# All 32 down products of a gated expert layer as split products, with GpSimd making four low parts, under new stage orders

## The chip, the cores and the metric

The kernel runs on one core of one Trainium2 chip. The metric is the device time of one execution in microseconds (us); lower is better. The engines are named as in the profile: PE (TensorE), PEld (its weight loads), DVE (VectorE), ACT (ScalarE), POOL (GpSimd) and SP (the queue that issues DMAs).

## The reference, cut to what matters

Four sequences of 256 tokens with 128 features pass through gated cross-attention (2 heads of 64, 256 context tokens of 96 features, the latents appended to keys and values), and then through a gated expert layer with a residual. The second part is what the change touches:

```python
def ffn(x, expert_sel, keys, values):            # x: normalised, 1024 tokens x 128
    sel_logits = jnp.einsum('nd,ed->ne', xt, expert_sel)
    gates = jax.nn.sigmoid(sel_logits)
    sel_val, sel_idx = jax.lax.top_k(gates, 4)   # of 32 experts
    gate_full = jnp.zeros_like(gates).at[jnp.arange(N)[:, None], sel_idx].set(sel_val)
    scores = jax.nn.relu(jnp.einsum('nd,edf->nef', xt, keys))      # 32 experts x 64
    scores = scores * gate_full[:, :, None]
    return jnp.einsum('nef,efv->nv', scores, values)
x = x + tanh(g_xattn) * xattn(ctx, layernorm(x), mask, ...)
x = x + tanh(g_ffn) * ffn(layernorm(x), expert_sel, keys, values)
```

Every gate is computed, all 32 experts are evaluated for all tokens, and gates outside the top four are zero.

## The kernel before, in words

Each engine runs one list of stages in the written order (`PE_ORDER`, `POOL_ORDER`, `DVE_ORDER`, `ACT_ORDER`); stages are tied together by semaphores. A stage name is followed by its index: a sequence (0 to 3) for `turn_in 2` or `select 3`, sequence and part for `row_max 1.0`, half and chunk for `up 0.7` and `down 1.3`.

**Attention.** For each sequence: statistics and normalisation (`stats_in`, `norm_in`, on DVE and ACT), transposes (`turn_in`), projections (`project`), per-head norms of queries and keys (`sum_qk`, `norm_qk`), transposes back (`turn_qk`, and on ACT rounded copies, `round_qk`), the score maxima (`row_max`: PE makes scores, DVE reduces them), the maxima moved to rows (`turn_max`), exponentials (`weights`: scores on PE, Exp on ACT), the weighted values (`attend`, two tiles per sequence), and on DVE the residual (`out_proj`), statistics and normalisation (`stats_mid`, `norm_mid`, `turn_mid`). `warm` is a matmul on an identity whose result nobody reads. `constants` on ACT makes a bf16 identity and the open part of the mask.

**Gates.** `select` makes 32 logits per token (PE), the top four and sigmoids (DVE), `turn_gates` transposes them (PE, ACT), and SP writes them to DRAM and reads each row back, broadcast over 64 partitions, into one of 6 slots (`gated`), one load per chunk.

**Expert layer.** The 2048 hidden columns are 16 chunks of 128, and the tokens two halves of 512: 32 chunks, n = 16*half + chunk. `up` on PE is a product of split operands: `product` adds low x high, high x low and high x high in three fp32r matmuls of 512 columns (L729, L730, L731). `up` on DVE (L543) applies ReLU and gate and writes the fp32 chunk to one of 3 slots of `hid`. For n >= WHOLE = 4, ACT's `split` (L706) writes its rounded high part `hid_hi` and DVE's `split` (L560) the difference `hid_lo`, in rings of 4 slots, and `down` is again a `product` with `v_hi`, `v_lo`. For n < 4 `down` is one plain fp32 matmul on `hid` (L921), which shows as two instructions. DVE may not overwrite a `hid` slot before the three older chunk's down product (n < 4) or both its parts (n >= 4) are done:

```python
def free_hid(n):
    if 0 <= n < WHOLE:
        dve.wait_ge(down_done, n + 1)
    elif n >= WHOLE:
        dve.wait_ge(hid_hi_ready, n - WHOLE + 1)
        dve.wait_ge(hid_lo_ready, n - WHOLE + 1)
```

PE's `up` uses three PSUM banks in turn, so `up` n waits for DVE's `up` n-3. `turn_res` adds the residual into the accumulator by a transpose before the first `down` of a half.

**POOL** makes the low parts of keys and values, four quarters each (L349), the mask (L344) and the biased residual (`add_bias`, L363). In the attention part the orders are written out by hand, as everywhere.

Of the kernel before, what the change touches and what calls it, by code (L numbers as in the profile page):

```python
# [33 lines left out]
WHOLE = 4
# [32 lines left out]
    select 3, up 0.11, down 0.7, up 0.12, down 0.8, up 0.13, turn_gates 3, down 0.9, up 0.14, up 0.15, down 0.10,  # L67
    down 0.11, up 1.0, up 1.1, down 0.12, turn_res 2, down 0.13, up 1.2, down 0.14, turn_res 3, up 1.3,
    down 0.15, up 1.4, up 1.5, down 1.0, up 1.6, down 1.1, up 1.7, up 1.8, down 1.2, down 1.3, up 1.9, down 1.4,
    down 1.5, down 1.6, up 1.10, up 1.11, down 1.7, up 1.12, up 1.13, down 1.8, down 1.9, up 1.14, up 1.15,  # L70
    down 1.10, down 1.11, down 1.12, down 1.13, down 1.14, down 1.15
# [4 lines left out]
"""
DVE_ORDER = """
    stats_in 0, norm_in 0, stats_in 1, scale_wo 0, norm_in 1, stats_in 2, sum_qk 0, norm_in 2, stats_in 3,
    norm_qk 0, sum_qk 1, norm_in 3, norm_qk 1, row_max 0.0, row_max 0.1, row_max 1.0, turn_max 0, sum_qk 2,
    row_max 1.1, norm_qk 2, sum_qk 3, turn_max 1, norm_qk 3, row_max 2.0, row_max 2.1, row_max 3.0, out_proj 0,  # L80
    turn_max 2, stats_mid 0, row_max 3.1, norm_mid 0, out_proj 1, turn_max 3, stats_mid 1, turn_mid 0,
# [10 lines left out]
    stats_in 0, norm_in 0, constants 0, stats_in 1, turn_in 0, norm_in 1, fold 0, project 0, stats_in 2,  # L92
    turn_in 1, sum_qk 0, vctx 0, vlat 0, norm_in 2, project 1, split_keys 0, turn_in 2, stats_in 3, vlat 1,
    turn_qk 0, sum_qk 1, round_qk 0, norm_in 3, vctx 1, turn_in 3, turn_qk 1, round_qk 1, vlat 2, vctx 2,
    split_keys 1, project 2, split_values 0, vlat 3, sum_qk 2, vctx 3, weights 0.0, project 3, turn_qk 2,
    sum_qk 3, round_qk 2, weights 0.1, split_keys 2, weights 1.0, turn_qk 3, round_qk 3, weights 1.1,
    split_keys 3, stats_mid 0, weights 2.0, weights 2.1, turn_mid 0, stats_mid 1, weights 3.0, select 0,
    turn_mid 1, split_values 1, turn_gates 0, select 1, weights 3.1, turn_gates 1, stats_mid 2, turn_mid 2,
    split_values 2, split_values 3, stats_mid 3, select 2, split 0.4, split 0.5, split 0.6, split 0.7,
    turn_mid 3, split 0.8, split 0.9, select 3, split 0.10, turn_gates 2, turn_gates 3, split 0.11, split 0.12,  # L100
    split 0.13, split 0.14, split 0.15, split 1.0, split 1.1, split 1.2, split 1.3, finish 0, split 1.4,
# [898 lines left out]
```

## Time and profile before

| what | value |
|---|---|
| median of 3 runs | 114.44 us (114.16 to 114.53) |
| the profiled execution | 113.83 us, of which the span is 112.0 us |
| busy of the span | PE 105.6, DVE 94.4, ACT 65.1, POOL 16.0 us |
| granted TensorE clock, mean | 0.995 of full |

The span runs from the first to the last instruction; 1.83 us of the profiled execution lie outside it. Busy shares are averages over two parts with different limits: the attention part ends at about 60.5 us with the last `attend`, the expert layer fills the rest.

### The profile page before, as it was taken

The numbers are of one execution on the slowest core, as the hardware profiler recorded it, in microseconds if no ns is written. First come the engines' busy times: TensorE is split into PE (matmuls) and PEld (weight loads), VectorE is DVE, ScalarE is ACT, GpSimd is POOL, SyncE is SP. The second block draws the span as 40 slices with busy tenths as digits, with TensorE's granted clock in tenths as the row PEclk, the third lists the DMA queues.
The fourth block names the chain that finished last, engine by engine and source line by source line (L and its number), as shares of the span: only waits on it lengthen the run. The fifth ranks groups of instructions, "written<-read, shape, count | busy, mean of one in ns | idle before, by whom it ended". The sixth has DMA issues, their size and how long they took to land.

```text
span 112.0 us, 2072 instructions
## 1 busy us (share of the span) xinstructions
PE 105.6 (94%) x644; PEld 85.4 (76%) x644; DVE 94.4 (84%) x307; ACT 65.1 (58%) x145; POOL 16.0 (14%) x27
## 2 busy tenths in 40 slices
...
DMA packets 7111, 12.78 MB, mean 114 GB/s; under 512 B 893, under 2 KB 2557, under 8 KB 6846
## 3 DMA queue, kind: packets, MB, share of 16 engines
...
HBM read 12.00 MB, written 0.66 MB: 113 GB/s over the span
## 4 chain that ended last, share of the span: by engine, by line
PE 79%; DVE 8%; ACT 7%; issue 3%; POOL 0%; DVEq 0%; POOLq 0%
PE bank L729 13%; PE bank L731 13%; PE bank L730 13%; PE bank L867 12%; PE bank L738 6%; PE bank L854 5%; PE bank L921 3%; PE bank L825 2%; DVE junk L453 2%; PE bank L852 2%; PE bank L788 2%; PE bank L813 1%; ACT cx L600 1%; PE bank L807 1%; PE bank L892 1%
## 5 line engine op out<-in xcount | busy, mean ns | idle before, releaser
L706 ACT ACTIVATE hid_hi<-keys 128x512 fp32r<-128x512 f32 x28 | 17.5, 630 | 18.5 <-DVE keys L543 15.3
L543 DVE SCALAR_TENSOR_TENSOR keys<-bank,inT 128x512 f32<-128x512 f32 x32 | 21.1, 685 | 1.3 <-issue 0.6
L560 DVE TENSOR_TENSOR hid_lo<-keys,hid_hi 128x512 fp32r<-128x512 f32 x28 | 18.7, 685 | 0.9 <-ACT hid_hi L706 0.6
L867 PE MATMUL bank<-vw,prob 128*128 128x129 f32 x128 | 15.8, 278 | 0.0
L867 PEld LDWEIGHTS bank<-vw,prob 128*128 128x128 f32 x128 | 14.8, 192 | 0.7 <-issue 0.7
L729 PE MATMUL bank<-xm_hi,k_lo 128*128 128x512 f32 x32 | 14.5, 454 | 0.0
L453 DVE CUSTOM_DVE_ANT_0 junk<-bank,mask_b 128x512 bf16<-128x512 f32 x16 | 10.4, 688 | 3.0 <-PE bank L825 3.0
L731 PE MATMUL bank<-xm_hi,k_hi 128*128 128x512 f32 x32 | 12.5, 391 | 0.0
L730 PE MATMUL bank<-xm_lo,k_hi 128*128 128x512 f32 x32 | 12.5, 390 | 0.0
L729 PE MATMUL bank<-hid_hi,v_lo 128*128 128x512 f32 x28 | 11.2, 399 | 0.0
L731 PE MATMUL bank<-hid_hi,v_hi 128*128 128x512 f32 x28 | 10.9, 391 | 0.0
L730 PE MATMUL bank<-hid_lo,v_hi 128*128 128x512 f32 x28 | 10.9, 390 | 0.0
L674 ACT ACTIVATE prob<-bank 128x512 f32<-128x512 f32 x16 | 8.6, 592 | 3.5 <-PE bank L854 3.4
L738 PE MATMUL bank<-ident 128*128 128x128 f32 x48 | 8.3, 327 | 1.5 <-POOL ident L330 1.5
L349 POOL TENSOR_TENSOR k_lo<-keys,k_hi 128x512 fp32r<-128x512 f32 x4 | 5.1, 1271 | 30.7 <-ACT k_hi L642 30.7
L738 PEld LDWEIGHTS bank<-ident 128*128 128x128 f32 x48 | 7.8, 241 | 1.7 <-POOL ident L330 1.5
L854 PE MATMUL bank<-qT,kT 64*128 64x256 f32 x64 | 9.1, 375 | 0.0
L729 PEld LDWEIGHTS bank<-xm_hi,k_lo 128*128 128x128 f32 x32 | 6.0, 188 | 2.0 <-issue 0.7
L730 PEld LDWEIGHTS bank<-xm_lo,k_hi 128*128 128x128 f32 x32 | 6.0, 189 | 1.9 <-issue 1.0
L349 POOL TENSOR_TENSOR v_lo<-values,v_hi 128x512 fp32r<-128x512 f32 x4 | 5.1, 1275 | 16.9 <-ACT v_hi L648 16.9
L731 PEld LDWEIGHTS bank<-xm_hi,k_hi 128*128 128x128 f32 x32 | 6.0, 188 | 1.3
L731 PEld LDWEIGHTS bank<-hid_hi,v_hi 128*128 128x128 f32 x28 | 5.3, 188 | 1.1
...
## 6 DMA issues: line engine op xcount, KB each, us to landing
...
```

What stands on the lines that cost most here:

```text
L349: pool.tensor_tensor(lo[:, part], src[:, part], hi[:, part].bitcast(F32), ALU.subtract).then_inc(lo_ready, 1)
L453: dve.tensor_tensor_reduce(junk[:, n % 2, :], bank_of(b, ROW_MAX + i)[:, :], mask_b[:, b, :], 1.0, SENTINEL, ALU.add, ALU.max, mx[:, b, i ...
L543: dve.scalar_tensor_tensor(hid[:, n % 3, :], bank[H_BANK[n % len(H_BANK)]][:, :], 0.0, gated[:, n % SLOTS, :], ALU.max, ALU.mult).then_inc ...
L560: dve.tensor_tensor(hid_lo[:, m % RING, :], hid[:, n % 3, :], hid_hi[:, m % RING, :].bitcast(F32), ALU.subtract).then_inc(hid_lo_ready, 1)
L674: act.activation(prob[:, b % 2, a, 2 * i:2 * i + 2, :], head_bank(b, a)[:, :].rearrange("p (t s) -> p t s", t=2), ACT.Exp).then_inc(prob_r ...
L706: act.activation(hid_hi[:, m % RING, :], hid[:, n % 3, :], ACT.Copy).then_inc(hid_hi_ready, 1)
L729: pe.matmul(o, ll, rh, start=start, stop=False)
L730: pe.matmul(o, lh, rl, start=False, stop=False)
L731: return pe.matmul(o, lh, rh, start=False, stop=stop)
L738: pe.matmul(bank[5][:, 0:P], ident[:, :], ident[:, :], start=True, stop=True)
L854: last = pe.matmul(o[a], kT[rows[a], b, keys_t], qT[rows[a], b, :], start=False, stop=True)
L867: last = pe.matmul(bank_of(b, OUT + t)[:, WOA * a:WOA * a + WOA], prob[:, b % 2, a, j, P * t:P * t + P], vw[:, b, j, a, :], start=(j == 0) ...
```

## The change: every chunk is split, and four low parts move to POOL

`WHOLE` becomes 0, so chunks 0.0 to 0.3 also get high and low parts and a three-matmul product. POOL makes the low part of every eighth chunk (0.5, 0.13, 1.5, 1.13), counted by a semaphore of its own; `wait_low` picks the semaphore. DVE thus makes 28 low parts as before, but two more of them in the first half and two fewer in the second. All four orders are new.

```diff
-WHOLE = 4
+POOL_EVERY, POOL_SLOT = 8, 5
+WHOLE = 0
...
+        def wait_low(engine, m):
+            pool_made = (m - POOL_SLOT) // POOL_EVERY + 1
+            if m % POOL_EVERY == POOL_SLOT:
+                engine.wait_ge(pool_lo_ready, pool_made)
+            else:
+                engine.wait_ge(hid_lo_ready, m + 1 - pool_made)
...
+            def split(h, c):                                  # gpsimd
+                n = EC * h + c
+                m = n - WHOLE
+                pool.wait_ge(hid_ready, n + 1)
+                pool.wait_ge(hid_hi_ready, m + 1)
+                if m >= RING:
+                    pool.wait_ge(down_done, n - RING + 1)
+                pool.tensor_tensor(hid_lo[:, m % RING, :], hid[:, n % 3, :], hid_hi[:, m % RING, :].bitcast(F32),
+                                   ALU.subtract).then_inc(pool_lo_ready, 1)
...
-                    dve.wait_ge(hid_lo_ready, n - WHOLE + 1)
+                    wait_low(dve, n - WHOLE)
...
-                    pe.wait_ge(hid_lo_ready, m + 1)
+                    wait_low(pe, m)
```

The parts of the orders that matter below (before, then after):

```diff
 PE_ORDER
-    turn_in 0, warm 13, warm 14, warm 15, warm 16, warm 17, warm 18, fold 0, project 0, turn_in 1, warm 19,
-    vlat 0, vctx 0, warm 20, project 1, turn_in 2, vctx 1, warm 21, vlat 1, warm 22, turn_qk 0, warm 23, vctx 2,
-    vlat 2, turn_in 3, row_max 0.0, turn_qk 1, vlat 3, row_max 0.1, row_max 1.0, project 2, turn_max 0, vctx 3,
-    row_max 1.1, weights 0.0, project 3, turn_max 1, turn_qk 2, weights 0.1, weights 1.0, row_max 2.0, turn_qk 3,
-    attend 0.0, row_max 2.1, weights 1.1, row_max 3.0, attend 0.1, turn_max 2, attend 1.0, row_max 3.1,
-    weights 2.0, attend 1.1, weights 2.1, turn_max 3, turn_mid 0, weights 3.0, select 0, attend 2.0, turn_mid 1,
-    weights 3.1, turn_gates 0, select 1, attend 2.1, turn_gates 1, attend 3.0, attend 3.1, turn_mid 2, up 0.0,
-    up 0.1, select 2, turn_res 0, turn_res 1, up 0.2, down 0.0, up 0.3, up 0.4, down 0.1, up 0.5, down 0.2,
-    up 0.6, down 0.3, up 0.7, up 0.8, down 0.4, turn_mid 3, down 0.5, turn_gates 2, up 0.9, down 0.6, up 0.10,
...
+    warm 13, turn_in 0, warm 14, warm 15, warm 16, warm 17, project 0, fold 0, warm 18, turn_in 1, warm 19,
+    vlat 0, project 1, vctx 0, turn_in 2, warm 20, warm 21, turn_qk 0, warm 22, vlat 1, vctx 1, row_max 0.0,
+    warm 23, vlat 2, vctx 2, row_max 0.1, turn_in 3, project 2, turn_qk 1, vctx 3, turn_max 0, vlat 3,
+    weights 0.0, row_max 1.0, project 3, weights 0.1, row_max 1.1, turn_qk 2, attend 0.0, turn_max 1, attend 0.1,
+    weights 1.0, row_max 2.0, turn_qk 3, weights 1.1, row_max 2.1, row_max 3.0, attend 1.0, turn_max 2,
+    row_max 3.1, attend 1.1, weights 2.0, turn_max 3, turn_mid 0, weights 2.1, weights 3.0, select 0, turn_mid 1,
+    attend 2.0, select 1, weights 3.1, attend 2.1, turn_gates 0, turn_gates 1, attend 3.0, attend 3.1, up 0.0,
+    turn_mid 2, up 0.1, select 2, turn_res 0, up 0.2, up 0.3, turn_res 1, down 0.0, up 0.4, up 0.5, down 0.1,
+    up 0.6, turn_gates 2, down 0.2, down 0.3, up 0.7, turn_mid 3, down 0.4, up 0.8, up 0.9, down 0.5, down 0.6,
...
+    up 1.14, down 1.10, up 1.15, down 1.11, down 1.12, down 1.13, down 1.14, down 1.15
 POOL_ORDER (after)
+    scale_bo 0, low_keys 0, mask 0, add_bias 0, low_values 0, low_keys 1, low_keys 2, low_keys 3, add_bias 1,
+    low_values 1, low_values 2, split 0.5, low_values 3, split 0.13, split 1.5, split 1.13
 DVE_ORDER
-    stats_mid 3, up 0.0, up 0.1, up 0.2, select 2, up 0.3, up 0.4, norm_mid 3, split 0.4, up 0.5, up 0.6, up 0.7,
...
+    stats_in 0, norm_in 0, stats_in 1, scale_wo 0, norm_in 1, stats_in 2, sum_qk 0, norm_in 2, norm_qk 0,
+    sum_qk 1, stats_in 3, row_max 0.0, norm_in 3, norm_qk 1, row_max 0.1, turn_max 0, sum_qk 2, row_max 1.0,
...
+    stats_mid 3, up 0.0, up 0.1, up 0.2, split 0.0, split 0.1, up 0.3, split 0.2, select 2, up 0.4, split 0.3,
+    norm_mid 3, up 0.5, split 0.4, up 0.6, turn_mid 3, up 0.7, split 0.6, up 0.8, up 0.9, split 0.7, split 0.8,
 ACT_ORDER (after)
+    stats_in 0, constants 0, norm_in 0, turn_in 0, stats_in 1, project 0, norm_in 1, fold 0, turn_in 1,
...
+    turn_qk 2, split_values 0, split_keys 3, round_qk 2, weights 1.0, turn_qk 3, round_qk 3, weights 1.1,
+    stats_mid 0, weights 2.0, turn_mid 0, stats_mid 1, weights 2.1, split_values 1, turn_mid 1, weights 3.0,
```

## Rows read from the trace of the kernel before

**Rows 1.** Busy time of each engine over the span, from the page.
```profile
PE 105.6 (94%) x644; PEld 85.4 (76%) x644; DVE 94.4 (84%) x307; ACT 65.1 (58%) x145; POOL 16.0 (14%) x27
```

**Rows 2.** One five-us stretch: length, busy PE, PEld, DVE, ACT, POOL, clock, DMA.
```profile
65.00:70.00 5.00, 5.00 (x19) 3.27 (x18) 4.72 (x20) 0.89 (x2) 0.00 (x0) 1.00 0.75 249
```

**Rows 3.** PE in order of time: start, length, line (idle before in brackets).
```profile
10.51 0.38 PE L746 MATMUL bank<-ident,xn 128*128 128x128 f32 x2
...
20.86 0.42 PE L749 MATMUL bank<-ident,cx 128*96 128x128 f32 x2 [0.49 <-ACT cx L600]
...
35.01 1.95 PE L867 MATMUL bank<-vw,prob 128*128 128x129 f32 x16
...
56.65 0.40 PE L892 MATMUL bank<-ident,gate 128*32 128x128 f32 x2 [0.38 <-DVE gate L534]
56.88 3.74 PE L867 MATMUL bank<-vw,prob 128*128 128x129 f32 x32
60.49 0.59 PE L875 MATMUL bank<-ident,xn 128*128 128x128 f32 x2
```

**Rows 4.** DVE in order of time, at the start of the expert layer.
```profile
63.05 1.26 DVE L543 SCALAR_TENSOR_TENSOR keys<-bank,inT 128x512 f32<-128x512 f32 x2
64.65 0.69 DVE L543 SCALAR_TENSOR_TENSOR keys<-bank,inT 128x512 f32<-128x512 f32 x1 [0.34 <-PE bank L731]
65.26 0.21 DVE L522 TENSOR_SCALAR logit<-bank 128x64 f32<-128x64 f32 x1
...
67.33 1.28 DVE L543 SCALAR_TENSOR_TENSOR keys<-bank,inT 128x512 f32<-128x512 f32 x2
68.53 0.15 DVE L496 SCALAR_TENSOR_TENSOR rs_mid<-rs_mid 128x2 f32<-128x2 f32 x1
...
69.63 0.69 DVE L560 TENSOR_TENSOR hid_lo<-keys,hid_hi 128x512 fp32r<-128x512 f32 x1
70.23 2.01 DVE L543 SCALAR_TENSOR_TENSOR keys<-bank,inT 128x512 f32<-128x512 f32 x3
72.16 1.28 DVE L560 TENSOR_TENSOR hid_lo<-keys,hid_hi 128x512 fp32r<-128x512 f32 x2
```

**Rows 5.** PE in order of time, in the expert layer.
```profile
69.79 1.02 PE L921 MATMUL bank<-keys,values 128*128 128x512 f32 x2
70.25 0.79 PE L729 MATMUL bank<-xm_hi,k_lo 128*128 128x512 f32 x1
70.88 0.40 PE L730 MATMUL bank<-xm_lo,k_hi 128*128 128x512 f32 x1
...
72.98 0.47 PE L729 MATMUL bank<-hid_hi,v_lo 128*128 128x512 f32 x1
...
101.32 0.39 PE L729 MATMUL bank<-xm_hi,k_lo 128*128 128x512 f32 x1
...
102.00 0.39 PE L729 MATMUL bank<-hid_hi,v_lo 128*128 128x512 f32 x1
```

**Rows 6.** ACT in order of time: an exponential pair, a rounded part, and the copies after key transposes.
```profile
36.24 0.71 ACT L661 ACTIVATE kT<-bank,vecs_x 128x512 f32<-128x512 f32 x1
36.81 0.45 ACT L665 ACTIVATE qT_hi<-qT 128x256 fp32r<-128x256 f32 x1
37.12 0.66 ACT L667 ACTIVATE kT_hi<-kT 128x512 fp32r<-128x512 f32 x1
38.53 1.09 ACT L674 ACTIVATE prob<-bank 128x512 f32<-128x512 f32 x2 [0.76 <-PE bank L854]
```

**Rows 7.** POOL in order of time: the mask, and two low parts of values.
```profile
17.62 1.04 POOL L344 TENSOR_SCALAR mask_b<-mask_u 128x1024 bf16<-128x1024 uint8 x1
...
62.10 2.52 POOL L349 TENSOR_TENSOR v_lo<-values,v_hi 128x512 fp32r<-128x512 f32 x2 [7.52 <-ACT v_hi L648]
```

**Rows 8.** DVE in order of time, beside the mask and after it.
```profile
17.65 1.02 DVE L384 SCALAR_TENSOR_TENSOR rs_in<-rs_in 128x4 f32<-128x4 f32 x1
...
19.69 0.17 DVE L384 SCALAR_TENSOR_TENSOR rs_qk<-rs_qk 128x12 f32<-128x12 f32 x1
```

More of the change, by code:

```diff
@@ L67 @@
[L67 to L71, printed above, removed]
+    warm 13, turn_in 0, warm 14, warm 15, warm 16, warm 17, project 0, fold 0, warm 18, turn_in 1, warm 19,
@@ new lines @@
+    attend 2.0, select 1, weights 3.1, attend 2.1, turn_gates 0, turn_gates 1, attend 3.0, attend 3.1, up 0.0,
+    turn_mid 2, up 0.1, select 2, turn_res 0, up 0.2, up 0.3, turn_res 1, down 0.0, up 0.4, up 0.5, down 0.1,
+    up 0.6, turn_gates 2, down 0.2, down 0.3, up 0.7, turn_mid 3, down 0.4, up 0.8, up 0.9, down 0.5, down 0.6,
+    up 0.10, down 0.7, select 3, up 0.11, up 0.12, down 0.8, up 0.13, turn_gates 3, up 0.14, down 0.9,
+    turn_res 2, turn_res 3, up 0.15, down 0.10, up 1.0, down 0.11, down 0.12, up 1.1, down 0.13, down 0.14,
@@ L72 @@
+    up 1.2, up 1.3, down 0.15, up 1.4, up 1.5, up 1.6, down 1.0, down 1.1, down 1.2, up 1.7, up 1.8, up 1.9,
+    down 1.3, down 1.4, up 1.10, down 1.5, up 1.11, down 1.6, down 1.7, down 1.8, up 1.12, up 1.13, down 1.9,
+    up 1.14, down 1.10, up 1.15, down 1.11, down 1.12, down 1.13, down 1.14, down 1.15
 """
 POOL_ORDER = """
-    low_keys 0, mask 0, low_keys 1, low_keys 2, scale_bo 0, add_bias 0, low_keys 3, add_bias 1, low_values 0,
-    low_values 1, low_values 2, low_values 3
+    scale_bo 0, low_keys 0, mask 0, add_bias 0, low_values 0, low_keys 1, low_keys 2, low_keys 3, add_bias 1,
@@ L76 @@
+    low_values 1, low_values 2, split 0.5, low_values 3, split 0.13, split 1.5, split 1.13
 """
 DVE_ORDER = """
[L78 to L81, printed above, removed]
@@ L87 @@
-    split 1.4, up 1.6, up 1.7, split 1.5, split 1.6, up 1.8, split 1.7, up 1.9, split 1.8, up 1.10, split 1.9,
-    up 1.11, split 1.10, up 1.12, up 1.13, split 1.11, split 1.12, up 1.14, up 1.15, split 1.13, split 1.14,
+    stats_in 0, norm_in 0, stats_in 1, scale_wo 0, norm_in 1, stats_in 2, sum_qk 0, norm_in 2, norm_qk 0,
+    sum_qk 1, stats_in 3, row_max 0.0, norm_in 3, norm_qk 1, row_max 0.1, turn_max 0, sum_qk 2, row_max 1.0,
+    norm_qk 2, sum_qk 3, row_max 1.1, norm_qk 3, turn_max 1, out_proj 0, row_max 2.0, stats_mid 0, row_max 2.1,
@@ new lines @@
+    row_max 3.0, norm_mid 0, turn_max 2, row_max 3.1, out_proj 1, stats_mid 1, turn_max 3, turn_mid 0,
+    norm_mid 1, turn_mid 1, select 0, select 1, out_proj 2, stats_mid 2, norm_mid 2, out_proj 3, turn_mid 2,
+    stats_mid 3, up 0.0, up 0.1, up 0.2, split 0.0, split 0.1, up 0.3, split 0.2, select 2, up 0.4, split 0.3,
+    norm_mid 3, up 0.5, split 0.4, up 0.6, turn_mid 3, up 0.7, split 0.6, up 0.8, up 0.9, split 0.7, split 0.8,
+    up 0.10, select 3, up 0.11, split 0.9, up 0.12, split 0.10, up 0.13, split 0.11, split 0.12, up 0.14,
@@ L91 @@
 ACT_ORDER = """
[L92 to L101, printed above, removed]
@@ L102 @@
-    split 1.5, split 1.6, split 1.7, split 1.8, split 1.9, split 1.10, split 1.11, split 1.12, split 1.13,
-    split 1.14, split 1.15
+    stats_in 0, constants 0, norm_in 0, turn_in 0, stats_in 1, project 0, norm_in 1, fold 0, turn_in 1,
+    stats_in 2, vlat 0, sum_qk 0, norm_in 2, split_keys 0, project 1, vctx 0, turn_qk 0, round_qk 0, turn_in 2,
+    sum_qk 1, stats_in 3, vlat 1, vlat 2, norm_in 3, vctx 1, vctx 2, turn_in 3, project 2, turn_qk 1, round_qk 1,
+    vctx 3, vlat 3, weights 0.0, sum_qk 2, project 3, weights 0.1, split_keys 1, split_keys 2, sum_qk 3,
@@ new lines @@
+    turn_qk 2, split_values 0, split_keys 3, round_qk 2, weights 1.0, turn_qk 3, round_qk 3, weights 1.1,
+    stats_mid 0, weights 2.0, turn_mid 0, stats_mid 1, weights 2.1, split_values 1, turn_mid 1, weights 3.0,
+    select 0, select 1, weights 3.1, split_values 2, turn_gates 0, turn_gates 1, stats_mid 2, turn_mid 2,
+    split 0.0, split 0.1, split 0.2, stats_mid 3, split 0.3, select 2, split 0.4, split 0.5, turn_mid 3,
+    split 0.6, split_values 3, split 0.7, split 0.8, split 0.9, select 3, split 0.10, turn_gates 2, turn_gates 3,
@@ L104 @@
+    split 0.11, split 0.12, split 0.13, split 0.14, split 0.15, split 1.0, split 1.1, split 1.2, split 1.3,
+    finish 0, split 1.4, split 1.5, split 1.6, split 1.7, split 1.8, split 1.9, split 1.10, split 1.11,
+    split 1.12, split 1.13, split 1.14, split 1.15
 """
```

11 lines of the change are left out of this document (5 added, 6 removed).

## The prediction, on record before the change was run

> **What bounds the kernel now.** First the page: PE is busy for 105.6 of 112.0 us and DVE for 94.4 [rows 1], so PE sets the end, with DVE close behind. The chain that ended last agrees: 79% of it is PE. POOL's 16.0 us leave room. Then PE in order of time. Up to the last `attend` (60.49) the idle times it shows are few: 0.49 us before the fourth `turn_in`, 0.38 before `turn_gates 1` [rows 3]. But its stages are worth less than the time they take: from 10.51 to 35.01, 24.5 us, their own costs add up to 21.8. I add 0.42 for a `turn_in`, 1.32 `project`, 0.87 `vlat` or `vctx`, 0.66 `turn_qk`, 0.46 `row_max`, 1.1 `weights`, 0.22 `warm`, each the distance between two starts in that timeline. So 2.7 us there are waits, written or smeared. From 35.01 to 60.49, 25.5 us, they add up to 24.4: 1.1 of waits.
>
> In the expert layer PE is full. A split product takes 0.68 us (101.32 to 102.00 [rows 5]); from 72.98, where `down 0.5` starts, to the end of the last product, 50 products (34.1) and four small stages fill everything. DVE has 0.60 us per chunk and operation (three in 70.23 to 72.16 are 1.93 with one handoff, pairs 1.20), and is 94% busy from 65 to 70 [rows 2]. `select` takes it 2.07 us (65.26 to 67.33), `norm_mid` 1.10 (68.53 to 69.63) [rows 4].
>
> **The change part by part.**
>
> *Four plain products become split.* The pair at 69.79 and the two matmuls behind it end the count at 70.88: 1.09 us, less 0.23 for one split matmul, is 0.86 [rows 5]. A split product is 0.68. PE gains 4 x 0.18 = 0.72 us. ACT gains 4 x 0.63 us of work, hidden, since it is mostly idle there.
>
> *DVE at the head of the expert layer.* This is what pays for it. DVE starts `up 0.0` at 63.05, after `out_proj 3`, `turn_mid 2` and `stats_mid 3`, all of them behind the last `attend`; the order of these is kept, so the distance (60.49 to 63.05) stays. `up 0.2` waits for PE today (0.34 us) and starts at about 64.5. From there the new order is a row of work with nothing to wait for until `split 0.4`: `up 0.2`, splits 0.0 and 0.1, `up 0.3`, split 0.2, `select 2`, `up 0.4`, split 0.3, `norm_mid 3`, `up 0.5`, split 0.4: nine operations at 0.60, 2.07 and 1.10, 8.6 us, and `split 0.4` is out at 73.15. PE needs it for `down 0.4` and starts that at 73.25. Behind it lie 28 down and 24 up products and four small stages (`select 3`, `turn_gates 3`, two `turn_res`). Before, PE had at 72.98 [rows 5] 27 down and 23 up products and five small stages behind it. So the new order is two products (1.36) minus one `turn_gates` (0.2) plus the 0.27 between 72.98 and 73.25 later: 1.4 us, the 0.72 included. Walked on PE, these are waits of 0.65 before `down 0.0` (it now needs a low part made behind `up 0.2`, where the plain product needed only `hid`), 0.5 before `turn_gates 2`, 0.2 before `down 0.3`, 0.7 before `down 0.4`, 0.2 more before `select 2`. After that DVE has spare room: by `up 1.3` the slot that PE asks for is 2 us old.
>
> *Late gate rows.* `turn_gates 3` comes at about 81.5 instead of 80.2, and the third load of the second half then lands near 90.3; the first product that needs it, `up 1.5`, starts at 92. Hidden, with 1 us of cover.
>
> *POOL's four low parts.* 2.52 us for two today [rows 7], so 1.27 each after ACT's 0.63: `split 0.5` is out about 2.0 us after `up 0.5`. DVE wants the slot for `up 0.8` 2.75 us after it (four operations and `turn_mid 3`), and 2.4 to 3.0 us later for the other two: hidden, cover 0.4 to 1.0 us. The trace has one warning. While POOL made the mask, DVE's `norm_in 3`, a 4-column operation on two SBUF inputs, took 1.02 us and ended with the mask; the like took 0.17 at 19.69 [rows 7, 8]. While POOL made low parts of values from 62.10 to 64.62, DVE's `up 0.0` and `up 0.1`, with one input in PSUM, kept 0.6 [rows 4, 7]. DVE's `split` reads two SBUF tensors, and no trace row shows it beside POOL. Bounds: 0, or four times 1.27 = 5.1 us of DVE. I take 0.3 us of DVE in the first half, covered by the 2 us of spare room there, and 0 on PE.
> The Trainium skill, "SBUF — State Buffer", section "Who interferes with whom", says that a DVE instruction with two SBUF inputs and a GpSimd instruction that reads SBUF exclude each other for a whole instruction. The 1.02 us agrees. By it each meeting costs one side up to an instruction; it speaks against moving these parts to GpSimd.
>
> *POOL's new queue.* `low_values 0` stands ahead of `low_keys 1` to `3` and waits for ACT's `split_values 0` (about 33.5); then five operations end at 39.8. The first reader of the last, `add_bias 1`, is `out_proj 2` (55), and `select 0` on ACT wants the keys' low parts at 49. Hidden. SP's list is unchanged.
>
> *The attention orders, first stretch (10.5 to `attend 0.0`).* `constants` goes ahead of `norm_in 0` on ACT and into the idle time there; `project 0` starts near 8.0 instead of 9.2, but `fold` (0.88) now follows it, so that only 0.1 is won by `turn_in 1`. The rest comes from `norm_qk 0` ahead of `stats_in 3` on DVE (13.65 instead of 15.04), so `turn_qk 0` and its rounding end at 17.7 instead of 20.0, and `row_max 0.0` goes at 18.0 instead of 21.2, ahead of `turn_in 3`. PE then has, up to `attend 0.0`, its own 21.8 us less 2.35 for stages that come later (`weights 1.0`, `row_max 2.0`, `turn_qk 3`, `turn_max 1`) and about 0.8 of waits: `attend 0.0` near 30.7.
>
> *Second stretch.* From there 24.4 + 2.35 own, and two new waits. `attend 1.0` needs `weights 1.1`, on ACT behind `turn_qk 3` and `round_qk 3`: after PE's transposes at 36.8, 0.95 + 0.8 + 1.08 [rows 6] is 39.6, PE is there at 39.0: 0.55. `weights 2.1` used to stand behind `attend 1.1`; now only `turn_max 3` and `turn_mid 0` separate it from `weights 2.0`, whose exponentials take 1.08 [rows 6]: 0.8. The 0.38 before `turn_gates 1` [rows 3] goes, as `select 1` comes ahead of `weights 3.1`. With 0.3 of small waits the last `attend` ends at 59.2 against 60.5: 1.3 us won.
>
> *Sum.* 112.0 - 1.3 + 1.4 = 112.1 of span. The profiled execution was 113.83, so 113.9 in its terms; the median of the runs shown is 114.44, 0.6 higher, and the forecast as such a median is 114.5. A measurement here tells about 0.3% (0.34 us) from no change.
>
> **The rivals.**
>
> *A: the attention orders win more.* My walk is long, and each handoff in it is an estimate. If the two new waits (0.55, 0.8) don't arise, because ACT and DVE run ahead, the last `attend` ends near 57.9 and the time is 114.5 - 1.3 = 113.2. The most that can be had there is all waits, 2.7 + 1.1. For it: PE is idle nowhere long. Against it: in both places the exponential pair has nothing to hide behind but 0.4 us.
>
> *B: the first stretch wins less (slower).* ACT is then as full as PE, and it got the same work. If `row_max 0.0` and `norm_qk 1` only swap which of ACT's stages is late, `attend 0.0` comes at 31.6 instead of 30.7; at less than 0.95 of gain left of the 1.3 the kernel becomes measurably slower. Losing 0.9 gives 115.4.
>
> *C: POOL and DVE meet.* One meeting at `split 0.6` behind `split 0.5`, or on `split 0.12`, costs DVE up to 1.27. At the second place it goes to the spare room. If it hits the first, where `down 0.5` and `up 0.9` are close, PE pays some 1.0: 115.5. The skill's rule above is this rival's; its chance is small because the trace of before gives room in the places that matter.
>
> *D: the head of the expert layer costs less.* If DVE's waits there were PE's in disguise, the kernel keeps the 0.72 of PE and the 1.3: 112.4. The rows leave little room for that, since the 8.6 us are bare operation times.
>
> **How the numbers follow.** Near cancellation (forecast, 113.9 to 115.0): 0.45, of which 0.11 faster by over 0.3%, 0.23 within and 0.11 slower. A: 0.23, D: 0.05, both faster. B: 0.18, C: 0.09, both slower. Faster 0.39, same 0.23, slower 0.38. The likeliest case's own range is 113.9 to 115.0; the range for 8 in 10 takes in most of A, B and C: 113.1 to 115.7.
>
> **What would show it.** The last `attend` ends near 59.2 (A: under 58.5, B: over 59.8). `row_max 0.0` at 18. PE waits 0.5 to 0.7 before `down 0.0`, `turn_gates 2` and `down 0.4`, and starts `down 0.4` 12.8 us after the last `attend` (D: under 12). L921 is gone, L560 still counts 28, POOL has four new operations of 1.27. A `split` on DVE that takes over 1 us beside POOL would be C. From `down 0.4` on PE has no wait over 0.3. I am wrong if `attend 0.0` doesn't come before 32, or if DVE isn't the engine PE waits for between 63 and 73.

## The result, and the profile after

| | before | after |
|---|---|---|
| median | 114.3 us (113.91 to 114.53, 4 runs) | 115.53 us (115.24 to 116.45, 4 runs) |
| the profiled execution / its span | 113.83 / 112.0 | 115.24 / 113.4 |
| ratio, 95% interval | | 1.0121 [1.0079, 1.0163] |

The change costs 1.2%. The forecast was 114.5, inside the 0.3% that can't be told from no change; the measured time lies in the range for 8 in 10 (113.1 to 115.7), near its upper end, and outside the 113.9 to 115.0 of the likeliest case: a gain and a loss were to cancel, and they didn't. Line numbers of PE, DVE and ACT code are 19 higher after the change (`product` L748 to L750, `attend` L886, DVE's `up` L562 and `split` L579, POOL's `split` L367).

The page gives the busy times:

```profile
PE 104.7 (92%) x648; PEld 85.6 (76%) x648; DVE 94.9 (84%) x307; ACT 66.5 (59%) x149; POOL 21.9 (19%) x31
```

PE is busy 0.9 us less than before [rows 1] in a span that is 1.4 longer: its own work fell, as the arithmetic on the products said (0.72), and its idle time grew by 2.3. Where they stand is seen on PE in order of time (start, length, line; in brackets the idle time before and what ended it):

```profile
18.10 0.50 PE L844 MATMUL bank<-kT_hi,qT_hi 64*128 64x512 f32 x2
...
31.36 0.91 PE L886 MATMUL bank<-vw,prob 128*128 128x129 f32 x6 [0.22 <-ACT prob L693]
...
40.54 1.13 PE L886 MATMUL bank<-vw,prob 128*128 128x129 f32 x8 [0.57 <-ACT prob L693]
...
47.45 0.28 PE L871 MATMUL bank<-shift_r,shift_l 33*128 33x256 bf16 x2 [0.71 <-ACT prob L693]
...
60.17 0.47 PE L748 MATMUL bank<-xm_hi,k_lo 128*128 128x512 f32 x1
...
62.48 0.25 PE L748 MATMUL bank<-sel_hi,xm_lo 128*128 128x32 f32 x1 [0.46 <-DVE xm_lo L531]
...
65.75 0.47 PE L748 MATMUL bank<-hid_hi,v_lo 128*128 128x512 f32 x1 [0.57 <-DVE hid_lo L579]
...
69.55 0.39 PE L911 MATMUL bank<-ident,gate 128*32 128x128 f32 x2
...
70.88 0.47 PE L748 MATMUL bank<-hid_hi,v_lo 128*128 128x512 f32 x1 [0.25 <-ACT hid_hi L725]
...
73.17 0.47 PE L748 MATMUL bank<-hid_hi,v_lo 128*128 128x512 f32 x1 [0.45 <-ACT hid_hi L725]
```

Five waits stand in the head of the expert layer: before `select 2` (62.48), `down 0.0` (65.75), `turn_gates 2` (69.55, where the start and not a bracket shows it), `down 0.3` (70.88) and `down 0.4` (73.17). The last two name ACT's high part, but that is the high part of the next chunk, which happened to end at about the same time. The one that `down 0.3` reads was made at 66.84 and the one that `down 0.4` reads at 70.17, as ACT in order of time shows:

```profile
66.84 0.63 ACT L725 ACTIVATE hid_hi<-keys 128x512 fp32r<-128x512 f32 x1 [0.75 <-DVE keys L562]
...
70.17 0.63 ACT L725 ACTIVATE hid_hi<-keys 128x512 fp32r<-128x512 f32 x1 [2.33 <-DVE keys L562]
72.47 0.63 ACT L725 ACTIVATE hid_hi<-keys 128x512 fp32r<-128x512 f32 x1 [1.67 <-DVE keys L562]
```

What ends both waits is DVE's low part: `split 0.3` runs from 70.05 to 70.73 and `down 0.3` starts at 70.88; `split 0.4` runs from 72.35 to 73.03 and `down 0.4` starts at 73.17. Behind 73.17 PE has no wait over 0.2 us.

The same stretch on DVE has no gap over 0.2 us:

```profile
62.93 2.08 DVE L562 SCALAR_TENSOR_TENSOR keys<-bank,inT 128x512 f32<-128x512 f32 x3
64.93 1.28 DVE L579 TENSOR_TENSOR hid_lo<-keys,hid_hi 128x512 fp32r<-128x512 f32 x2
66.13 0.68 DVE L562 SCALAR_TENSOR_TENSOR keys<-bank,inT 128x512 f32<-128x512 f32 x1
66.73 0.68 DVE L579 TENSOR_TENSOR hid_lo<-keys,hid_hi 128x512 fp32r<-128x512 f32 x1
67.33 0.21 DVE L541 TENSOR_SCALAR logit<-bank 128x64 f32<-128x64 f32 x1
...
69.44 0.69 DVE L562 SCALAR_TENSOR_TENSOR keys<-bank,inT 128x512 f32<-128x512 f32 x1
70.05 0.68 DVE L579 TENSOR_TENSOR hid_lo<-keys,hid_hi 128x512 fp32r<-128x512 f32 x1
...
72.35 0.68 DVE L579 TENSOR_TENSOR hid_lo<-keys,hid_hi 128x512 fp32r<-128x512 f32 x1
```

This is the row of work of the prediction; `split 0.4` is at 72.35.

**One mark for both parts.** The last `attend` is followed by other stages in the two kernels (a transpose at 60.49 [rows 3], `up 0.0` at 60.17), so these starts aren't the same mark: with the changed attention part and the old stage behind it (an experiment below) the transpose starts at 60.37. DVE's `up 0.0` is the same operation in both, behind the last `attend` and the same DVE stages. It starts at 63.05 before [rows 4] and 62.93 after: attention won 0.1 us. From there to the end of the span it is 112.0 - 63.05 = 48.95 before and 113.4 - 62.93 = 50.47 after: the expert part lost 1.5. I call this **the tail** and give it for every run; spans are printed to 0.1 us.

### The profile page after: what moved, and what is told of

Its sections match the earlier page's. It is cut to its first block, busy times and chain, and to the rows that moved or that the text cites. A ratio compares the mean times of both kernels' runs of the same rounds, so it can differ in the third digit from the quotient of the medians.

```text
span 113.4 us, 2104 instructions
## 1 busy us (share of the span) xinstructions
PE 104.7 (92%) x648; PEld 85.6 (76%) x648; DVE 94.9 (84%) x307; ACT 66.5 (59%) x149; POOL 21.9 (19%) x31
## 4 chain that ended last, share of the span: by engine, by line
PE 68%; DVE 13%; ACT 12%; issue 3%; DVEq 0%; POOL 0%; POOLq 0%
PE bank L748 13%; PE bank L749 12%; PE bank L750 12%; PE bank L886 10%; PE bank L873 5%; PE bank L757 5%; ACT prob L693 4%; PE bank L778 3%; PE bank L871 2%; ACT hid_hi L725 2%; ACT cx L619 1%; DVE hid_lo L579 1%; DVE keys L562 1%; DVE x_mid L495 1%; DVE x_mid L500 1%
## 5 line engine op out<-in xcount | busy, mean ns | idle before, releaser
L725 ACT ACTIVATE hid_hi<-keys 128x512 fp32r<-128x512 f32 x32 | 20.0, 631 | 20.0 <-DVE keys L562 15.7
L562 DVE SCALAR_TENSOR_TENSOR keys<-bank,inT 128x512 f32<-128x512 f32 x32 | 21.4, 684 | 1.9 <-PE bank L750 1.0
L579 DVE TENSOR_TENSOR hid_lo<-keys,hid_hi 128x512 fp32r<-128x512 f32 x28 | 18.9, 692 | 0.5 <-DVE keys L562 0.3
L886 PE MATMUL bank<-vw,prob 128*128 128x129 f32 x128 | 15.8, 278 | 0.8 <-ACT prob L693 0.8
L886 PEld LDWEIGHTS bank<-vw,prob 128*128 128x128 f32 x128 | 14.8, 191 | 1.9 <-issue 1.9
L748 PE MATMUL bank<-hid_hi,v_lo 128*128 128x512 f32 x32 | 12.8, 399 | 1.3 <-ACT hid_hi L725 0.7
L367 POOL TENSOR_TENSOR hid_lo<-keys,hid_hi 128x512 fp32r<-128x512 f32 x4 | 5.7, 1425 | 42.2 <-ACT hid_hi L725 33.3
L748 PE MATMUL bank<-xm_hi,k_lo 128*128 128x512 f32 x32 | 13.0, 407 | 0.0
L750 PE MATMUL bank<-xm_hi,k_hi 128*128 128x512 f32 x32 | 12.5, 390 | 0.0
L750 PE MATMUL bank<-hid_hi,v_hi 128*128 128x512 f32 x32 | 12.5, 390 | 0.0
L749 PE MATMUL bank<-hid_lo,v_hi 128*128 128x512 f32 x32 | 12.5, 390 | 0.0
L748 PEld LDWEIGHTS bank<-hid_hi,v_lo 128*128 128x128 f32 x32 | 6.0, 188 | 3.3 <-issue 1.4
L750 PEld LDWEIGHTS bank<-xm_hi,k_hi 128*128 128x128 f32 x32 | 6.0, 188 | 1.3
L750 PEld LDWEIGHTS bank<-hid_hi,v_hi 128*128 128x128 f32 x32 | 6.0, 188 | 1.3
L748 PEld LDWEIGHTS bank<-xm_hi,k_lo 128*128 128x128 f32 x32 | 6.0, 188 | 1.2
```

The source lines that it names most:

```text
L367: pool.tensor_tensor(hid_lo[:, m % RING, :], hid[:, n % 3, :], hid_hi[:, m % RING, :].bitcast(F32), ALU.subtract).then_inc(pool_lo_ready, 1)
L562: dve.scalar_tensor_tensor(hid[:, n % 3, :], bank[H_BANK[n % len(H_BANK)]][:, :], 0.0, gated[:, n % SLOTS, :], ALU.max, ALU.mult).then_inc ...
L579: dve.tensor_tensor(hid_lo[:, m % RING, :], hid[:, n % 3, :], hid_hi[:, m % RING, :].bitcast(F32), ALU.subtract).then_inc(hid_lo_ready, 1)
L725: act.activation(hid_hi[:, m % RING, :], hid[:, n % 3, :], ACT.Copy).then_inc(hid_hi_ready, 1)
L748: pe.matmul(o, ll, rh, start=start, stop=False)
L749: pe.matmul(o, lh, rl, start=False, stop=False)
```

## The experiments

Ratios are to the kernel before, on the same chip, with 95% intervals.

**The expert part alone, and the attention part alone.** The first kernel has the orders of before up to the last `attend` and the changed code and orders behind it; the second has the changed attention orders on all engines and the expert layer of before:

```diff
 PE_ORDER of the expert part alone, against the changed kernel
-    warm 13, turn_in 0, warm 14, warm 15, warm 16, warm 17, project 0, fold 0, warm 18, turn_in 1, warm 19,
...
-    attend 2.0, select 1, weights 3.1, attend 2.1, turn_gates 0, turn_gates 1, attend 3.0, attend 3.1, up 0.0,
+    turn_in 0, warm 13, warm 14, warm 15, warm 16, warm 17, warm 18, fold 0, project 0, turn_in 1, warm 19,
...
+    weights 3.1, turn_gates 0, select 1, attend 2.1, turn_gates 1, attend 3.0, attend 3.1, up 0.0, turn_mid 2,
```

> The kernel before up to the last attend, with the expert part of the change alone (all chunks split, POOL's four low parts, its orders). Theory (DVE's row of work behind out_proj 3 sets when PE may start down 0.4, and the rest follows): the last attend ends near 60.5 as before, down 0.4 starts about 12.8 us after it, and the time is 1.6 us above the kernel before (ratio 1.014). Rival (the loss comes from the attention orders, which place DVE and ACT work badly for what follows): ratio under 1.005.

> The changed kernel up to the last attend, with the expert part of the kernel before (four plain products, no low part on POOL). Theory: the last attend ends 0.3 us earlier than before and nothing is lost behind it, ratio 0.997 (0.3 us under the kernel before). Rival (attention orders at fault): ratio over 1.007.

The expert part alone gives 115.66 us, 1.0129 [1.0087, 1.0171], the attention part alone 114.5, 1.001 [0.9977, 1.0042], where 0.3 us won was expected. In PE's timeline the first shows the same waits as the changed kernel:

```profile
65.90 0.47 PE L748 MATMUL bank<-hid_hi,v_lo 128*128 128x512 f32 x1 [0.57 <-DVE hid_lo L579]
...
73.33 0.47 PE L748 MATMUL bank<-hid_hi,v_lo 128*128 128x512 f32 x1 [0.46 <-ACT hid_hi L725]
```

Its tail is 113.6 - 63.08 = 50.5, that of the changed kernel. So the whole measured loss is in the expert part, and the attention orders win nothing that can be measured. The second kernel has a tail of 49.56, 0.6 longer than before with the same expert orders. In DVE's timeline it shows a wait that neither before nor after has:

```profile
62.94 1.25 DVE L542 SCALAR_TENSOR_TENSOR keys<-bank,inT 128x512 f32<-128x512 f32 x2
65.23 0.69 DVE L542 SCALAR_TENSOR_TENSOR keys<-bank,inT 128x512 f32<-128x512 f32 x1 [1.04 <-DMA inT<-gate_rows]
```

The third gate row was late by 1.04 us; the last experiment comes back to it.

**Only the first four splits taken back (the plain head).**

```diff
-POOL_EVERY, POOL_SLOT = 8, 5
-WHOLE = 0
+POOL_EVERY, POOL_SLOT = 8, 1
+WHOLE = 4
 DVE_ORDER (ACT_ORDER likewise)
-    up 0.2, split 0.0, split 0.1, up 0.3, split 0.2, select 2, up 0.4, split 0.3, norm_mid 3, up 0.5, split 0.4,
+    up 0.2, up 0.3, select 2, up 0.4, norm_mid 3, up 0.5, split 0.4,
```

> The changed kernel, all orders kept, but chunks 0.0 to 0.3 are plain fp32 products again and their splits are gone from DVE and ACT; POOL keeps its four. Theory: DVE's row of work is 4 x 0.60 = 2.4 us shorter, PE gives 4 x 0.18 = 0.72 us back, the waits ahead of down 0.0, turn_gates 2, down 0.3 and down 0.4 (about 2 us in all) go: the time falls by 1.2 to 1.6 us against the changed kernel, to a ratio of 0.998 to 1.002 against the kernel before. Rival (POOL's four low parts collide with DVE's and cost the time): they are still there, so the ratio stays at 1.010 or more.

Measured: 114.22 us, 1.000 [0.9974, 1.0025], tail 49.33. PE's waits before `down 0.0`, `down 0.3` and `down 0.4` are gone; `down 0.4` starts at 72.03, 1.14 earlier than after. POOL still makes its four low parts here, of the same chunks. By the tail the four splits at the head are 1.1 of the 1.5 us; 0.4 stays with the rest of the change (new orders, POOL's parts), less than the medians resolve. The 4 x 0.18 us that PE wins on the splits is inside this balance. It also shows that POOL's four parts, under these orders, bring nothing that can be measured while the head is plain, though DVE has four parts fewer than before.

**More of the head to POOL.** Two kernels give POOL also the low parts of 0.2 and 0.3, or of 0.2 alone (`POOL_MADE = (2, 5, 13, 21, 29)`); those leave DVE's order:

```diff
-POOL_EVERY, POOL_SLOT = 8, 5
+POOL_MADE = (2, 3, 5, 13, 21, 29)
-            if m % POOL_EVERY == POOL_SLOT:
+            if m in POOL_MADE:
 POOL_ORDER
-    low_values 2, split 0.5, ...
+    low_values 2, split 0.2, split 0.3, split 0.5, ...
```

> The changed kernel with the low parts of chunks 0.2 and 0.3 on POOL too. Theory: DVE's row of work is 1.2 us shorter, POOL makes 0.2 behind split 0.1 and 0.3 beside select 2, where DVE reads no two SBUF tensors of size; down 0.4 starts 0.9 to 1.2 us earlier, ratio near 1.003. Rival (POOL and DVE hold each other up for whole instructions): DVE's split 0.1 or the up behind it takes over 1.2 us, and the gain is under 0.4 us, ratio 1.009 or more.

> The changed kernel with only the low part of chunk 0.2 on POOL beside the four. In e4, with 0.2 and 0.3 there, a tensor_scalar of select 2 took 1.11 us while POOL made 0.3. Theory (POOL's low part of 0.3 holds that DVE operation for the whole instruction): with 0.3 back on DVE the operation takes 0.18 again, and DVE's row of work is 0.6 shorter than in the changed kernel against 0.3 in e4: down 0.4 starts at 72.5 to 72.7, earlier than e4's 73.0 with one part fewer on POOL. Rival (the 1.11 us has another cause, such as a late exponential from ACT): it stays long, and down 0.4 starts at 73.0 or later.

With two more: 115.29 us, 1.0094 [1.006, 1.0129], tail 50.25, so 0.2 won where 1.2 us of DVE were taken away; 0.9 to 1.2 were expected. The gain is as small as the rival said, but the meeting is at another place than it named. POOL's timeline and DVE's show where the rest went:

```profile
65.92 1.55 POOL L366 TENSOR_TENSOR hid_lo<-keys,hid_hi 128x512 fp32r<-128x512 f32 x1 [8.51 <-ACT hid_hi L724]
67.73 1.29 POOL L366 TENSOR_TENSOR hid_lo<-keys,hid_hi 128x512 fp32r<-128x512 f32 x1 [0.25 <-ACT hid_hi L724]
```

```profile
67.96 1.11 DVE L550 TENSOR_SCALAR keys<-keys 128x64 f32<-128x64 f32 x1
```

A 64-column `tensor_scalar` of `select 2`, with one SBUF input, takes 1.11 us instead of 0.18 and ends with POOL's operation: 0.9 of the 1.2 given back. With one more: 115.72 us, 1.0087 [1.0045, 1.0129]. In its profile `select 2` is undisturbed, as expected. From DVE's `up 0.2` to PE's `down 0.4` it is 65.29 to 73.54, 8.25 us, against 8.84 in the changed kernel (64.33 to 73.17) and 8.57 with two more (64.43 to 73.00): the row of work is 0.6 shorter, as expected. But the third gate row held `up 0.2` by 1.04 us, so `down 0.4` still came later than the 72.5 to 72.7 expected, and the time doesn't differ measurably from the changed kernel.

**The order at the head.** `select 2` behind `split 0.4`, so that the chunks come out sooner:

```diff
 PE_ORDER
-    up 0.6, turn_gates 2, down 0.2, ... down 0.5, down 0.6,
+    up 0.6, down 0.2, ... down 0.5, turn_gates 2, down 0.6,
 DVE_ORDER (ACT_ORDER likewise)
-    split 0.2, select 2, up 0.4, split 0.3, norm_mid 3, up 0.5, split 0.4, up 0.6,
+    split 0.2, up 0.4, split 0.3, norm_mid 3, up 0.5, split 0.4, select 2, up 0.6,
```

> The changed kernel with select 2 on DVE (2.07 us) moved behind split 0.4 and turn_gates 2 on PE behind down 0.5; every operation is still there. Theory (which operations stand ahead of split 0.4 in DVE's row sets the start of down 0.4): down 0.4 starts near 71.1 instead of 73.2, up 0.9 then waits for DVE's up 0.6, whose time does not move, and about 0.9 of the 2.1 us stay won: ratio 1.003 to 1.006. Rival (DVE's total work in the first half is the bound, whatever its order): the waits come back behind down 0.4 in full, ratio 1.010 or more.

Measured: 116.83 us, 1.0201 [1.0158, 1.0245]; tail 50.72, 0.25 longer than after. (In this profiled execution DVE's `up 0.0` is 0.85 us late as well, at 63.78; the first `turn_in` was already 1.15 late. The edit doesn't reach that far, so how much of the median it explains is open.) In PE's timeline the waits before `turn_gates 2`, `down 0.3` and `down 0.4` are gone (that before `down 0.0` stays, 0.56), `down 0.4` starts at 72.27, and a longer wait stands behind it:

```profile
74.96 0.51 PE L748 MATMUL bank<-xm_hi,k_lo 128*128 128x512 f32 x1 [1.06 <-DVE keys L562]
```

The theory's gain of 0.9 fell and the rival holds: in the first half DVE's total is the limit, and the order only chooses which product waits for it.

**POOL's four parts given back to DVE.**

```diff
-POOL_EVERY, POOL_SLOT = 8, 5
+POOL_MADE = ()
 DVE_ORDER (and so for split 0.13, split 1.5, split 1.13)
-    norm_mid 3, up 0.5, split 0.4, up 0.6, turn_mid 3, up 0.7, split 0.6,
+    norm_mid 3, up 0.5, split 0.4, up 0.6, turn_mid 3, up 0.7, split 0.5, split 0.6,
```

> The changed kernel with POOL's four low parts back on DVE, each ahead of the next chunk's. Theory (DVE's total work up to the end of the first half sets the loss): DVE gets two more parts there, 1.2 us, of which the 0.3 us that collisions with POOL cost come back: the time rises by 0.3 to 0.9 us against the changed kernel, ratio 1.015 to 1.021. Rival (POOL's low parts cost more in collisions than they take off DVE): the time falls, ratio 1.010 or less.

Measured: 117.31 us, 1.0278 [1.0229, 1.0327]; tail 51.36, 0.9 longer than after. The median rose by 1.8 us, more than expected and more than the tail. The other 0.9 of the profiled span lies ahead of DVE's `up 0.0` (63.84), where the edit doesn't reach: the first `turn_in` of this execution was 1.24 late. By the tail POOL's help is worth 0.9 us here, the upper end of what was expected, with the rest of the change in place; with the plain head no such gain shows.

**POOL's operations beside a full DVE.** The kernel before with 20 POOL operations of the same form between 64.6 and 95.2 us, whose result nobody reads:

```diff
+            for i in range(20):
+                pool.wait_ge(junk_done, i) if i else None
+                pool.tensor_tensor(pool_junk[:, :], x[:, 0:4, :].rearrange("p t d -> p (t d)"),
+                                   x[:, 4:8, :].rearrange("p t d -> p (t d)"), ALU.subtract).then_inc(junk_done, 1)
```

> The kernel before with 20 more tensor_tensor of 512 columns on POOL behind its own list, two SBUF inputs, results that nobody reads, about 1.3 us each from 64.6 to 91. Theory (a DVE operation with two SBUF inputs, as split is, and one on POOL exclude each other): DVE's splits in that stretch take up to 1.9 instead of 0.69 us, its ups (one input in PSUM) stay at 0.69, PE waits for DVE and the time is 2 us or more above the kernel before. Rival (they share): splits stay under 0.8 us, ratio within 1.003.

Measured: 124.03 us, 1.0835 [1.0785, 1.0886]: some 0.5 us for each operation, more than the 2 us in all that was expected at least, though not all of it is DVE being held: the profile also has a late gate row (1.3 us of DVE) and a mean granted clock of 0.83 between 75 and 85 us, behind a stretch (65 to 75) in which PE was busy 6.9 of 10 us. By line (xcount | busy us, mean ns | idle before, releaser):

```profile
L565 DVE TENSOR_TENSOR hid_lo<-keys,hid_hi 128x512 fp32r<-128x512 f32 x28 | 23.2, 845 | 0.3 <-ACT hid_hi L711 0.2
L548 DVE SCALAR_TENSOR_TENSOR keys<-bank,inT 128x512 f32<-128x512 f32 x32 | 20.9, 680 | 1.5 <-DMA inT<-gate_rows 1.3 <-PE bank L736 0.2
...
L506 DVE TENSOR_SCALAR xn<-x_mid,mv_mid,rs_mid 128x128 f32<-128x128 f32 x8 | 4.5, 608 | 0.1
```

DVE's `split` (two SBUF inputs) rises from 0.69 to 0.85 on average, though only 10 of the 28 ran beside POOL (two of these take 3.01 at 77.77); `up` (one input in PSUM, one in SBUF) stays at 0.68. The form that pays most is `norm_mid`'s `tensor_scalar`, all in SBUF, two of which take 2.72 us in DVE's timeline where they took 0.60:

```profile
72.73 2.72 DVE L506 TENSOR_SCALAR xn<-x_mid,mv_mid,rs_mid 128x128 f32<-128x128 f32 x2
```

**The attention part, first and second stretch.** Three kernels looked for its missing 1.2 us. The mask at the head of POOL's order, once in the kernel with the plain head and once in the kernel before, tests what the mask's meeting with DVE costs (at `sum_qk 1` after, 0.75 us for 0.17; at `norm_in 3` before [rows 8]):

```diff
 POOL_ORDER, plain head
-    scale_bo 0, low_keys 0, mask 0, add_bias 0, low_values 0,
+    mask 0, scale_bo 0, low_keys 0, add_bias 0, low_values 0,
 POOL_ORDER, kernel before
-    low_keys 0, mask 0, low_keys 1,
+    mask 0, low_keys 0, low_keys 1,
```

> e3_plain_head with the mask first in POOL's order. In the changed kernel the mask runs from 16.27 to 17.31, and a tensor_scalar of sum_qk 1 on DVE (one SBUF input) takes 0.75 us there instead of 0.17. Theory (POOL's mask shuts DVE out): the mask now runs near 7.7 to 8.8, where DVE waits for ACT, the 0.58 us at sum_qk 1 goes, row_max 0.0 on DVE starts up to 0.6 earlier and the last attend ends 0 to 0.4 us earlier; the time is that of e3 or up to 0.3 us less. Rival (the 0.75 us was a wait of another kind): it stays.

> The kernel before with the mask first in POOL's order and nothing else. Theory: the 1.02 us operation of norm_in 3 at 17.65 falls to 0.17, norm_in 3 is out 0.85 us earlier; ACT is full there, so that little of it reaches PE: ratio 0.996 to 1.000. If the new place shuts DVE out at norm_in 1 (8.47) instead, ratio up to 1.003.

The first: 114.24 us, 1.0004 [0.9976, 1.0031]. In DVE's timeline the hold-up at 16.6 is still there, and a second one has come at 7.6:

```profile
7.63 0.68 DVE L428 TENSOR_SCALAR var_in<-mv_in 128x2 f32<-128x2 f32 x1
...
16.59 0.85 DVE L450 TENSOR_SCALAR ms<-ss 128x12 f32<-128x12 f32 x1
```

The mask's old place was taken by `add_bias`, a POOL `tensor_tensor`, which holds DVE as well: the expected detail was missed. The second: 114.74 us, 1.0048 [1.0017, 1.0079], slower, and above both ranges expected. There the mask holds DVE's 2-column `tensor_scalar` of `stats_in 1`:

```profile
7.67 1.00 DVE L411 TENSOR_SCALAR var_in<-mv_in 128x2 f32<-128x2 f32 x1
```

`scale_wo` comes late, and PE waits 0.46 at `fold` (9.04). The hold-up at `norm_in 3` [rows 8] is gone and wins nothing: the fourth `turn_in` waits for ACT by the same 0.49 as before.

The third, on the kernel with the plain head, hides the exponentials of `weights 2.0` behind `attend 1.1`:

```diff
-    row_max 3.1, attend 1.1, weights 2.0, turn_max 3,
+    row_max 3.1, weights 2.0, attend 1.1, turn_max 3,
```

> e3_plain_head with one stage moved on PE: weights 2.0 ahead of attend 1.1, as it was before, so that its exponentials run beside attend 1.1. Theory: the 0.71 us wait before weights 2.1 goes and the last attend ends 0.4 to 0.7 us earlier (59.5 to 59.8); but the third gate row lands when it lands, so DVE's wait for it grows unless the gates come earlier too, and the time falls by 0.3 to 0.6 us against e3, ratio 0.995 to 0.998. Rival (the gate rows set the start of the expert layer): the last attend is earlier, the time is that of e3.

Measured: 115.4 us, 1.0083 [1.0055, 1.0112], where the kernel without the edit had 1.000; the tail is the same (49.33). PE's timeline has two longer waits, on the other engine:

```profile
44.11 0.28 PE L869 MATMUL bank<-shift_r,shift_l 33*128 33x256 bf16 x2 [0.59 <-DVE shift_r L481]
...
49.88 0.28 PE L869 MATMUL bank<-shift_r,shift_l 33*128 33x256 bf16 x2 [1.00 <-DVE shift_r L481]
```

The 0.7 wait for ACT was traded for 1.6 of waits for DVE's `turn_max`, 0.9 lost, where 0.4 to 0.7 won were expected. (DVE's `up 0.0` is 1.30 later than in the kernel without the edit; 0.42 of that is already there at `attend 0.0`, 31.78 for 31.36, ahead of the edit.) Nothing runs ahead there.

**The gate rows.** The attention part alone once more, with the gates of the first half sent off sooner, to see what the late row costs:

```diff
 PE_ORDER
-    select 0, turn_mid 1, attend 2.0, select 1, weights 3.1, attend 2.1, turn_gates 0, turn_gates 1,
+    turn_mid 1, select 0, attend 2.0, select 1, attend 2.1, turn_gates 0, turn_gates 1, weights 3.1,
 ACT_ORDER
-    weights 3.1, split_values 2, turn_gates 0, turn_gates 1,
+    turn_gates 0, turn_gates 1, weights 3.1, split_values 2,
```

> The kernel with the attention part of the changed kernel and the expert part of the kernel before, with the gates of sequences 0 and 1 sent off sooner: on PE turn_mid 1 ahead of select 0, and weights 3.1 behind turn_gates 1; on ACT the two gate copies ahead of the exponentials 3.1. Theory (the earlier end of attention isn't cashed in because the gate rows for the expert layer are loaded at 59.1 us in every kernel, and the third row lands when it lands): turn_gates 1 goes near 55.4 instead of 56.5, the loads are issued near 58.1, DVE has no wait over 0.3 us for the third gate row before up 0.2 (1.04 before), PE's wait before up 0.8 (0.21) goes, and the span falls from 112.5 to about 112.0 or a little under, the time to 0.995 to 0.999 of the kernel before. Rival (the landing depends on what shares the DMA engines, not on the time of issue; or PE is full anyway): the third row still lands after 64.5, or it lands sooner and the span stays at 112.3 to 112.6, ratio 1.000 to 1.003. The last attend should end where it did, 60.4, within 0.2.

Measured: 115.83 us, 1.0138 [1.0097, 1.0179], slower, for a reason that I had missed. First SP's queue, then DVE, then PE:

```profile
57.93 3.87 SPq L314 DMA_DIRECT2D inT<-gate_rows  x6
```

```profile
64.60 1.25 DVE L542 SCALAR_TENSOR_TENSOR keys<-bank,inT 128x512 f32<-128x512 f32 x2
66.21 0.69 DVE L542 SCALAR_TENSOR_TENSOR keys<-bank,inT 128x512 f32<-128x512 f32 x1 [0.35 <-PE bank L730]
```

```profile
58.37 3.81 PE L866 MATMUL bank<-vw,prob 128*128 128x129 f32 x32 [1.26 <-ACT prob L673]
```

The loads are issued 1.2 us earlier, at 57.93, DVE no longer waits for a row, and the tail is 49.0, as in the kernel before and 0.55 under that of the attention part alone: in these profiled executions the late row costs about that. That the row landed sooner isn't shown: `up 0.2` came at 66.21, and a row landing at 65.23, as before, wouldn't have held it either. But the first `attend` of sequence 3 needs the exponentials of both parts, and with `weights 3.1` right ahead of it nothing hides the second pair: 1.26 us of PE, and DVE's `up 0.0` 1.7 later.

## Why the prediction was right or wrong, step by step

**The expert part: right, in mechanism, place and size.** Predicted 1.4 us lost, measured 1.5 (tail 50.47 against 48.95), of which 1.1 goes with the four splits (the plain head). DVE's row from `up 0.0` to PE's `down 0.4` was predicted at 10.2 us (63.05 to 73.25) and took 10.24 (62.93 to 73.17). The waits predicted at 0.65, 0.5, 0.2 and 0.7 are 0.57, about 0.3, 0.25 and 0.45; that before `select 2` grew by about 0.4, where 0.2 was predicted. So the sum is right while single waits are off by up to 0.25 both ways. L921 is gone, L579 counts 28. That this part is the whole measured loss is shown by the expert part alone (1.0129) and by the plain head (1.000); that DVE's total in the first half, not its order, sets it, by the `select` experiment and by POOL's parts given back.

**The attention part: the term that was mis-sized.** "1.3 us won" measured 0.1. `row_max 0.0` came at 18.10 as forecast (18.0), and the two new waits were right (0.57 and 0.71 for 0.55 and 0.8). What failed is the allowance of "about 0.8 of waits" up to `attend 0.0`: it came at 31.36, not 30.7. From 18.10 to 31.36 the stages' own costs by my table sum to 12.3 of 13.3 us, of which the profile shows 0.45 as idle; 10.51 to 18.10 has 0.4 more over its table. So some 1.4 us of waits where I allowed 0.8, spread over 28 stages. The second stretch gave 0.5 away in the same manner (31.57 us to DVE's `up 0.0` where 31.1 was forecast). The allowance had no row behind it. The wait share that this stretch had before (2.7 of 24.5) would have given 2.4, too much by 1.0. Over both stretches together the waits hardly changed: 3.8 of 50.0 us before (the prediction's 2.7 and 1.1), 3.7 of 49.9 after (10.51 to the 60.37 above, with the same 46.2 of own costs). The new orders moved them from the first stretch (2.7 to 1.4) to the second (1.1 to 2.3). Why the sum stayed is open.

**Rival B is half of what happened.** `attend 0.0` came at 31.36, which is 0.7 of the 0.9 that it named; the other 0.5 was lost in the second stretch, which no rival had. Together, losing 1.2 of the 1.3 gives 115.7, measured 115.53. That B's price for the whole fits is in part luck. Its ground, that ACT is as full as PE and got the same work, is seen in the windows, before and after (length; busy PE, PEld, DVE, ACT, POOL; clock, DMA), but no run took work off ACT there, so the cause is argued and not shown:

```profile
10.00:35.00 25.00, 23.76 (x158) 18.34 (x157) 21.94 (x82) 23.83 (x62) 3.59 (x3) 1.00 0.15 60
10.00:35.00 25.00, 24.54 (x170) 20.09 (x169) 21.58 (x82) 23.45 (x62) 4.45 (x4) 1.00 0.16 66
```

Rival A didn't happen, as the two new waits arose; `weights 2.0` sent ahead shows that DVE's `turn_max` would have been the next to wait for. Rival D fell with the plain head: what DVE holds up there is PE's loss.

**Rival C (POOL beside DVE): small in the changed kernel.** The low parts took 1.43 us on average, not 1.27. POOL's timeline, and DVE's:

```profile
85.25 1.56 POOL L367 TENSOR_TENSOR hid_lo<-keys,hid_hi 128x512 fp32r<-128x512 f32 x1 [8.93 <-PE bank L750]
95.86 1.55 POOL L367 TENSOR_TENSOR hid_lo<-keys,hid_hi 128x512 fp32r<-128x512 f32 x1 [9.06 <-ACT hid_hi L725]
105.80 1.30 POOL L367 TENSOR_TENSOR hid_lo<-keys,hid_hi 128x512 fp32r<-128x512 f32 x1 [8.39 <-ACT hid_hi L725]
```

```profile
96.40 0.69 DVE L562 SCALAR_TENSOR_TENSOR keys<-bank,inT 128x512 f32<-128x512 f32 x1
97.00 0.96 DVE L579 TENSOR_TENSOR hid_lo<-keys,hid_hi 128x512 fp32r<-128x512 f32 x1
```

Both sides can pay: POOL's operation at 95.86 meets a `split` already running and takes 0.3 longer, and the next `split`, at 97.00, waits 0.27 for POOL's end at 97.4. PE has no wait there. The experiments with more POOL work show that this was luck of the places.

**What no step had.** The earlier end of attention isn't passed on whole: the gate rows are issued at 59.06 to 59.15 both before and after, because the second sequence's gates leave at the same time, and in some executions the third row lands late enough to hold DVE's `up 0.2` by 1.0 to 1.3 us. In the expert orders of before this cost 0.55; what it costs behind the changed orders wasn't isolated, and the changed kernel's own profile has no such wait. With the plain head it costs nothing: DVE's timelines of that kernel and of the one with `weights 2.0` ahead, both with a tail of 49.33, show a wait for the row in the first, and in the second one of much the same size for `down 0.0`, whose `hid` slot `up 0.3` needs:

```profile
65.53 1.39 DVE L560 SCALAR_TENSOR_TENSOR keys<-bank,inT 128x512 f32<-128x512 f32 x2 [1.30 <-DMA inT<-gate_rows]
...
67.53 0.69 DVE L560 SCALAR_TENSOR_TENSOR keys<-bank,inT 128x512 f32<-128x512 f32 x1 [1.11 <-PE bank L938]
```

What decides when that row lands is open.
